# A new order of all steps and a new bank plan, with the time of each change of PE's tile mode counted

## The reference, cut to what matters

```python
x = x + tanh(g_xattn[0]) * L0_xattn(layernorm(x), ctx, ctx, ...)   # plain attention
x = x + tanh(g_ffn[0])   * L0_ffn(layernorm(x), ...)    # gelu of a linear map for the 192 best rows of 256
x = x + tanh(g_xattn[1]) * L1_xattn(ctx, ctx, layernorm(x), ...)   # plain attention
x = x + tanh(g_ffn[1])   * L1_ffn(layernorm(x), ...)    # 8 gated experts (top 2) and a shared one of twice the width
x = x + tanh(g_xattn[2]) * L2_xattn(layernorm(x), ctx, ...)        # causal attention
x = x + tanh(g_ffn[2])   * L2_ffn(layernorm(x), ...)    # 8 experts of 512 hidden units (top 2) and a shared one
x = x + tanh(g_xattn[3]) * L3_xattn(layernorm(x), ctx, ctx, ...)   # only the 51 best queries of each head
x = x + tanh(g_ffn[3])   * L3_ffn(layernorm(x), ...)    # rows and weight rounded to a 6-bit grid, then linear
```

## Time and profile before

| | |
|---|---|
| time, median of 3 runs | 957.2 us (955.71 to 961.45) |
| span of the profiled execution | 952.6 us |
| PE busy | 873.0 us (92%), 7,897 matmul records |
| PEld busy | 604.0 us (63%) |
| DVE busy | 712.2 us (75%) |
| ACT busy | 639.3 us (67%) |
| POOL busy | 497.5 us (52%) |
| chain that ended last | PE 64%, DVE 16%, POOL 7%, ACT 6%, issue 5% |

### The profile page before, as it was taken

The page is one execution under the profiler, slowest core; times in us unless marked ns, Lnnn a source line. Parts: engine busy times, 40 slices in busy tenths (PEclk is TensorE's granted clock), DMA queues, the critical chain, the costliest instruction groups (busy, mean ns, idle before and its releaser), DMA issues.

```text
span 952.6 us, 22448 instructions
## 1 busy us (share of the span) xinstructions
PE 873.0 (92%) x7897; PEld 604.0 (63%) x7897; DVE 712.2 (75%) x2174; ACT 639.3 (67%) x1460; POOL 497.5 (52%) x627
## 2 busy tenths in 40 slices
PE   6798889999999999899987999999999999999963
PEld 3344347855799987478533365746588987887522
DVE  7997988878543378987998899897745357656887
ACT  2786667767774645798674767777797448777841
POOL 6446555775962234655366265557772525533172
PEclk7897999999999999999998899999999999999997
DMA  5433241221100010002102021111110010000000
GB/s 156 111 96 86 73 111 43 77 64 37 28 23 23 14 39 3 21 24 63 36 21 74 20 66 32 32 41 30 33 41 1 18 35 1 19 20 18 20 3 24
DMA packets 67519, 39.93 MB, mean 42 GB/s; under 512 B 8263, under 2 KB 65376, under 8 KB 67408
## 3 DMA queue, kind: packets, MB, share of 16 engines
q1 hardware_dynamic: 62608, 30.44, 12.5%
q0 software_dynamic: 2208, 6.78, 2.6%
q10 hardware_dynamic: 2592, 1.26, 0.5%
HBM read 11.12 MB, written 1.05 MB: 13 GB/s over the span
## 4 chain that ended last, share of the span: by engine, by line
PE 64%; DVE 16%; POOL 7%; ACT 6%; issue 5%; DMA 1%; SPq 0%; DVEq 0%; ACTq 0%; POOLq 0%
PE banks L1062 12%; PE banks L1053 12%; PE banks L886 8%; PE banks L1022 6%; DVE mx L1364 6%; PE banks L868 4%; PE banks L845 4%; PE banks L831 3%; PE banks L1032 3%; ACT probs L743 3%; POOL h L603 3%; PE banks L991 2%; PE banks L824 2%; POOL rn L650 2%; PE banks L931 2%
## 5 line engine op out<-in xcount | busy, mean ns | idle before, releaser
L1364 DVE TENSOR_REDUCE mx<-banks 128x4 f32<-128x1024 f32 (+1 forms) x240 | 284.1, 1217 | 25.9 <-PE banks L845 18.9
L743 ACT ACTIVATE probs<-banks 128x512 f32<-128x512 f32 (+1 forms) x512 | 258.7, 582 | 53.3 <-PE banks L868 50.2
L796 ACT ACTIVATE probs<-banks,b_sb 128x256 f32<-128x256 f32 x288 | 118.0, 474 | 72.8 <-PE banks L1053 71.3
L886 PE MATMUL banks<-probs,v_aug 128*9 128x256 f32 (+1 forms) x2048 | 149.1, 373 | 7.2 <-ACT probs L743 5.9
L1062 PE MATMUL banks<-w_sb,probs 128*128 128x128 f32 x1152 | 140.6, 277 | 0.2 <-ACT probs L743 0.2
L1062 PEld LDWEIGHTS banks<-w_sb,probs 128*128 128x128 f32 x1152 | 134.9, 192 | 5.7 <-issue 2.5
L1053 PE MATMUL banks<-hT,w_sb 128*128 128x256 f32 x576 | 137.4, 382 | 0.1
L596 POOL TENSOR_TENSOR rstd<-veps,mhalf 128x2 f32<-128x2 f32 x64 | 46.2, 723 | 165.5 <-DVE veps L1311 164.8
L650 POOL TENSOR_TENSOR rn<-ss,mhalf 128x32 f32<-128x32 f32 x16 | 88.0, 5500 | 53.2 <-DVE ss L1159 52.9
L1053 PEld LDWEIGHTS banks<-hT,w_sb 128*128 128x128 f32 x576 | 104.4, 190 | 14.7 <-DVE xs L1235 0.8
L845 PE MATMUL banks<-k_st,q_st 64*128 64x256 bf16 (+1 forms) x1024 | 93.4, 277 | 14.3 <-DVE mx L1364 4.6
(11 more groups left out here) (195 smaller groups left out, 1451.5 us busy)
## 6 DMA issues: line engine op xcount, KB each, us to landing
k_st<-k_parts SPq DMA_DIRECT2D x192, 64.0 KB, 2.1
q_st<-q_parts SPq DMA_DIRECT2D x186, 64.0 KB, 2.1
w_sb<-in_w POOLq DMA_DIRECT2D x16, 256.0 KB, 3.3
fc_sb<-in_fc POOLq DMA_DIRECT2D x6, 256.0 KB, 4.1
x_in<-in_x SPq DMA_DIRECT2D x8, 128.0 KB, 4.3
cT<-in_ctxT SPq DMA_DIRECT2D x8, 128.0 KB, 2.7
out_x<-xs SPq DMA_DIRECT2D x8, 128.0 KB, 2.0
q_st<-mT SPq DMA_DIRECT2D x32, 16.0 KB
```

Of the source, the lines that this page charges most:

```text
L743: nc.scalar.activation(probs[s][:, part % UNIT_RING, 2 * a:2 * a + 2, 0:n], b_bank(w, a + 1)[:, 0:2 * n].rearrange("p (j q) -> p j q", j=2 ...
L796: ins = nc.scalar.activation(hid[s][:, part % UNIT_RING, c, :], b_bank(w, half + 1)[:, j * ROWS:(j + 1) * ROWS], ACT.Gelu, bias=b1_sb[:, p ...
L886: ins = nc.tensor.matmul(c_bank(b, l, u // 4)[VW * i:VW * i + VR, g % 2, q0:ROWS], v_aug[s][:, t, 4 * g + i, :], probs[s][:, u % UNIT_RING ...
L1364: nc.vector.tensor_reduce(mx[s][:, r, :, hp0:hp0 + n], banks[:, first:first + 2, :].rearrange("p a (n k) -> p a n k", n=n), AX.X, ALU.max) ...
```

## The change

Both strings of digits are replaced, `TURNS_TAKEN` and `BANKS_TAKEN`; no other line differs. There is the same number of steps, instructions, bytes and waits of every kind. The ACT_TABLE_LOADs of ACT, which the build puts in where the kind of function changes, are 43 in place of 45. What made the digits, a planner outside the kernel that now counts the time of each change of tile mode, is not in the file. The first lines of each:

```diff
 TURNS_TAKEN = """
-0002012001311331020003100000202003000101213111001100110011001101200210202020120120023101212121122322
+0001103021231201000032100002330000000110211301101100101010111100200120202001301202022220111212113123
...
 BANKS_TAKEN = """
-1023546012345671002345671023456701253406712503456703124056341203567401236740123406123456701234560123
+3046170124523674130167512645672345106723115674023154670523404536072314562371674521673401673254013567
...
```

More of the change, by code:

```diff
@@ L152 @@
-6774465467557477776777776777777547775545667766765775774645666776764767767457444466764576774455554454
-4665477676556566656654656565665564666464665777777567656756676657757776746766547556645776777776657477
-4577577767767675775776574777677657475765474564757775647646777647546477767777745757654677
+0001103021231201000032100002330000000110211301101100101010111100200120202001301202022220111212113123
+1102121020130313311001201022112021320032000012122201030332332231231102021121112331212323323100133300
+2210330123033302020323232013232222010313200033000120101201031100130303133003033310003201331101121201
@@ new lines @@
+2113212113222210002100001100221223221220322321220311230221212330012300322022131010021110102013110210
+1002211212210213322102111221212221031303310130330331213003320222303222330222103333101213213310103133
+0100202201201200221201102333331300121032121032123301212100212203012212200130303312213100120012302001
+1022013333000210111100010001211111200211000321201013222021201011001022010000020002101120212131111211
+2011102020101001120321210113111112122203130210300212202202332020202012202320003230210311211222311002
@@ new lines @@
+2223200020120310303001002320100030313000103031000123213002032203313112132130203313013221301211233111
+3111311212211121133131031113233103112323230230333300001220331232220131002330031001023311311031103044
+1114111343333412341132222553353525424343433454432342224432434444343222352224535234223555444544552554
+4452455253435423324433244554335453554254543343545223545454455334434424525435543343354235253323532345
+3323353223532455226536335335335363356545644443635443445343354656364364464646644664464366464635644534
@@ new lines @@
+5334436336466663334363656566644636454563366465546345665633776447766545665656444447654666455566744646
+4445575765755757767757774457775744766445455755756777467657776675457775554655575564577555765745576575
+7754765555466565456746676564654666446746677776776475646466647565557647466467445666565466746645766666
+6666667566754456676544745754676757747554544755554667556776747677646775476576744445447676444455767555
+4464465454474755664744557547774547557656654747454476676575767757564476754577777665657474766776756464
@@ L155 @@
+7575546775675544644457446675454455644445777645467775545765756657557675545547465677554647455777756466
+6466667564744665747456774744466676765656777677646555767666466574577446754654456775554677554566574766
+7446464577567577747674477776777775774676776766767755776656776467677577665445646557776447744545554546
+6646745475674556655665566555646656646646677576765765776676656767675776677746755645674747577676745657
+7774747777577477775767677656477745577476474756577766564565777774656776777777656574657477
 """
@@ L214 @@
 BANKS_TAKEN = """
-1023546012345671002345671023456701253406712503456703124056341203567401236740123406123456701234560123
[L216 to L233, removed]
+3046170124523674130167512645672345106723115674023154670523404536072314562371674521673401673254013567
+3456017402534012356147230514763024615234756246023571452341562437025416234016234670541234750163427016
@@ new lines @@
+4672346743206754120537463215642376450167230456307467142501476537432014532701237456013274523107145701
+5263472501423164523016427452301745671245036704521037612504356120437502143502347160524310761352076352
+4576123045623145601427360512367031567201546720123451206703402167214016376234015623470132645720175426
+1052451024561304612540764210674276027361523643165413412634012643056201576340153274105261374210526410
+3524167052461352745301657241650421706417365417352140612456701253467125043016745201452367045671234057
@@ new lines @@
+2605346721543671205731052376104762304703472763402731456012435612456123547623450176234515623472567172
+1034651201627637142350764317625140243710273514703250435213042571327564312046723502367153401267521461
+2401256743012345670324531231675423545612075621237601456730124517042670145236752312407430124573601263
+7245731624352063125704511245123450145120456712756312437560423701453601734561037126546712465301425632
+1756013276542034563201564723705613047564125637042360562416532406542370156245602356012345607127063124
@@ new lines @@
+5603710345612753016245316230145672403672013505674235047635620312576045627430127356103215672350167234
+0533417563213741560234125603403246013542037650145712416756071205601245670124562310456120560143243651
+2746501346701675342601273462071264031724021753042451571243670367213407671043167310672341074526451730
+5634150234167320457106324105641207352047125073642510301235641273456127037651342657341202570673125673
+4372645173054123764502375604237053641230423154326752301423750613425073460213456012365046231610326450
@@ L234 @@
+1462143051720653012407563425671250346123456041345251063430531054132350761405372154375723451675134766
+710672345101673545260317620415732415374020176350426135470
 """
```

## The result

The changed kernel takes 968.4 us (median of 4 runs, 965.45 to 975.35), the kernel before beside it 957.2: ratio 1.0109, 95% interval 1.0062 to 1.0155. So it is about 1% slower, 8 to 11 us, and outside the range of 942 to 967. The forecast was a small gain.

The account below looks back on a forecast made before the run. PE was taken to bound 50 to 475 and 550 to 900 us, DVE the rest. Terms -1.4 - 2.1 - 1.9 - 0.9 + 0.5 - 0.5 + 3.4 = -2.9 us from 957.2 gave 954 us, range 942 to 967.

Parts of the forecast that it names:

- Price of a mode change: On PE, each change of tile mode costs 0.10 us; 14 fewer changes give -1.4 us.
- The waits named: PE's waits at turns: three in PE-bound stretches, together -1.9 us; batch 5's in the DVE-bound middle, -0.9 us.
- The -0.5 at the end: Near the end, three turns ahead of three affine3 remove PE's 0.47 us wait for ACT's copy: -0.5 us.
- the -2.1 for short chains: Missing PE work between the two PE steps of short chains falls from 82.5 to 80.4 us: -2.1 us.
- the 0 for the ACT tables: On ACT, two fewer table loads of 1.283 us gain 0; -2.6 us if ACT had been waited for.
- Start: +0.5: At the start, first maxima tile comes 1.5 to 3 us later, some turns and norms earlier: +0.5 us, between -1 and +3.
- +3.4 for the PE-bound stretches: Banks retaken too early there: missing time grows by 6.8 us, half taken as paid, +3.4, bounds 0 and +6.8.
- Rival (b): Banks taken too early decide: 16.5 us extra missing time paid in full, DVE-bound stretches as well; 967 us, chance 0.16.
- my static count: Bank takes with less PE work than the reading time; after maxima tiles 26 before, 51 after, missing 6.0 to 16.8 us.
- What would show it: Signs in the changed profile: PE idle 27 to 31 us in PE-bound stretches, named turn waits shorter, clock not falling there.

Follow-up runs that it names:

- the probe: Kernel before with one extra one-column matmul in each of 72 hidden steps: whole-array 975.8 us, 64-row tile (144 mode changes more) 994.6 us.
- f5: Changed order, each output's bank chosen anew by the read times in the changed kernel's trace; 954.7 us, ratio to the kernel before 0.9920.
- i4: Changed order, all banks chosen by the later read times of two traces, the changed kernel's and f5's; ratio to the kernel before 0.9956.
- h2: Order of the kernel before, banks chosen by the read times of its own trace; ratio to the kernel before 1.0006.
- e4: Kernel before with one step moved, the query of batch 0 behind the keys of batch 1; ratio to the kernel before 1.0021.
- i3: Changed kernel with f5's banks only from 70 to 476 and 595 to 901 us, the PE-bound stretches; ratio to the kernel before 1.0039.
- h4: Changed kernel with f5's banks in the first 96 steps (55 us) only; ratio to the kernel before 1.0038.
- i1: Changed kernel with f5's banks from 70 us on only, its own banks before that; ratio to the kernel before 0.9972.
- i2: Changed kernel with f5's banks only in the middle stretch, 484 to 601 us; ratio to the kernel before 1.0073.
- e3: Changed order, each output given the bank longest free by a count of PE's work with fixed reader times; 983.5 us, ratio to the kernel before 1.0235.
- h3: Order of the kernel before, banks that leave 31.8 us missing by its trace in place of 12.4; ratio to the kernel before 1.0109.

## Why the prediction was wrong, point by point

**Price of a mode change: right, a little small.** In the changed kernel's trace sixteen matmuls of line 1062 take 1.78 us ahead of a whole-array step and 1.88 ahead of the 9 rows of line 1047:

```profile
282.26 1.95 PE L1062 MATMUL banks<-w_sb,probs 128*128 128x128 f32 x16
284.14 0.71 PE L1047 MATMUL banks<-b_sb,resid 9*128 9x128 f32 x4
...
288.34 1.95 PE L1062 MATMUL banks<-w_sb,probs 128*128 128x128 f32 x16
290.12 0.60 PE L898 MATMUL banks<-cT,wqk 128*128 128x256 f32 x2
```

With the probe's 0.13, 14 changes are worth 1.8 us and not 1.4. The Trainium skill, TensorEngine Tiling (Array Packing), section Key Properties, says that a change of tiling mode drains the engine; the probes agree that it costs, and put it at 0.13 us.

**The waits named: right.** The turns that waited 1.37, 0.60, 0.86 and (the one in the middle) 1.82 us in the earlier trace rows, and the long wait of the earlier trace rows, in order of time:

```profile
79.97 0.44 PE L824 MATMUL banks<-ident,h 128*128 128x128 f32 x2 [0.58 <-POOL h L603]
...
222.33 0.44 PE L824 MATMUL banks<-ident,h 128*128 128x128 f32 x2
...
535.69 0.44 PE L824 MATMUL banks<-ident,h 128*128 128x128 f32 x2 [0.72 <-POOL h L603]
...
678.83 0.38 PE L824 MATMUL banks<-ident,h 128*128 128x128 f32 x2
...
956.76 1.12 PE L824 MATMUL banks<-ident,h 128*128 128x128 f32 x4 [7.60 <-POOL h L645]
...
961.75 0.71 PE L1070 MATMUL banks<-w3T,hT 128*128 128x128 f32 x4 [0.47 <-ACT hT L674]
```

The first three fell to 0.58, 0 and 0, the middle one to 0.72: 0.79 + 0.60 + 0.86 + 1.10 = 3.4 us less, where 1.9 + 0.9 = 2.8 was forecast. The one near the end stayed (8.08, now 7.60). The -0.5 at the end came too: from the turn that ended this wait to the end of PE's last matmul it took 6.4 us before (the row below is its last) and takes 5.7, though a wait of 0.47 for ACT's copy is still there.

```profile
947.93 1.69 PE L1070 MATMUL banks<-w3T,hT 128*128 128x128 f32 x8
```

All terms but the banks made -6.3 us. f5 against the kernel before is -0.8%, -7.7 us (interval -4.5 to -10.7), i4 -4.2; both have fewer bank waits than the kernel before as well. Against h2, whose waits are nearest to theirs, they are -8 and -5 us. So the sum of the order's terms fits, though no run tells them apart: the -2.1 for short chains and the 0 for the ACT tables were not tested alone.

**Start: +0.5, measured about +2** (e4, 1.0021, 0 to 4 us by its interval; 1.2 us of lag in f5). Within its bounds of -1 and +3.

**Banks: the step that failed.** The text took +3.4 for the PE-bound stretches, "since a bank wait is free where PE would wait for a chain anyway", and nothing for the others, since "most are where DVE sets the pace". Measured against f5 the changed banks cost 16 us (against i4 12.7). f5's own waits are 5.7 us fewer than in the kernel before; the 13.9 us by which the waits grew from the kernel before are, at 0.7 to 0.9, some 10 to 12 us, about three times the term. In the PE-bound stretches i3 gives 4.7 us, inside the bounds of 0 and 6.8 and not to be told from the 3.4 that I took. At the start h4 and i1 give 5 us where the sum had nothing. The reason is in the rows: where DVE sets the pace, its work is what PE writes. A tile whose bank is still queued at DVE can only be written once DVE has read it, and then DVE has nothing for the time of writing. DVE-bound is no cover for a wait of PE on DVE's own input. This is shown for the start; for the middle, i2's 1.4 us leaves it open, and the end was not tried.

**Rival (b) came nearest**: full payment, in the DVE-bound stretches as well, 967 us. It had 0.16 because I took the missing time of my static count at face value and then halved it; the measured waits grew by 13.9 us, near its 16.5. Its time is 1.4 us from the measured one; that all of it is paid in full is more than the runs show. The upper bounds of the forecast's own terms, added up, come to +13 us or 970, so the range of 967 was cut below them.

**What would show it**: a wait between the second and third tile came (1.00 us); PE's idle time in the PE-bound stretches was 34.9 us, between the 27 to 31 of the forecast and the 40 of (b); the clock stayed at 0.98 and 1.00 there. The turns of batch 6 and batch 0 waited 0 and 0.58 us, under the 0.3 and 1.0 named. The forecast was to be wrong if the waits in the PE-bound stretches moved by more than 8 us or the clock fell in one of them. Neither happened, they rose by 4.9, and the forecast was wrong all the same: the test looked where the sum had put the banks' price and not at the start, where the sum had put none.

## To carry to other kernels

When a buffer or bank plan changes, count for each reuse how long the last reader takes to get to it in a trace, its queue included, and price the missing time at most of its length (here 0.7 us for each, over twelve kernels), also where the reader is the bound: it starves if its writer waits for it. A plan by distance or by fixed reader times can look better and be worse (e3, a loss of 2.4% in place of 1%); a plan by the read times of the order's own trace turned a loss of 1% into a gain of 0.8%, and a second such plan into 0.4%, with not one step moved. Where the banks were well spread already, it won nothing (h2).

## What was unexpected of the hardware

Part of the lag in the changed kernel's profile need not be work of the change. Between 120 and 160 us the granted clock was 1.00 in the profiled execution of the kernel before, 0.83 and 0.91 in that of the changed kernel, and the same 0.83 and 0.91 in h3, which has the order of the kernel before. i2 runs the same instructions on the same banks as the changed kernel up to 485 us. Four tables by stretch, before, changed, h3, i2:

```profile
120.00:140.00 20.00, 17.01 (x167) 8.97 (x166) 18.09 (x51) 13.84 (x31) 12.57 (x19) 1.00 0.43 111
140.00:160.00 20.00, 18.80 (x194) 12.34 (x195) 15.37 (x32) 14.36 (x34) 6.97 (x11) 1.00 0.15 33
```

```profile
120.00:140.00 20.00, 16.96 (x162) 8.37 (x162) 16.14 (x48) 13.16 (x29) 10.05 (x15) 0.83 0.36 90
140.00:160.00 20.00, 17.26 (x168) 9.81 (x168) 14.10 (x38) 12.87 (x29) 4.95 (x8) 0.91 0.30 82
```

```profile
120.00:140.00 20.00, 16.70 (x145) 8.55 (x146) 15.60 (x39) 12.51 (x27) 9.05 (x14) 0.83 0.34 88
140.00:160.00 20.00, 17.95 (x178) 9.76 (x177) 14.14 (x44) 13.43 (x31) 4.25 (x7) 0.91 0.26 72
```

```profile
120.00:140.00 20.00, 16.73 (x173) 9.16 (x174) 18.36 (x51) 14.79 (x32) 11.74 (x19) 1.00 0.40 100
140.00:160.00 20.00, 18.00 (x192) 10.26 (x191) 15.55 (x47) 13.66 (x32) 6.52 (x10) 1.00 0.29 78
```

By the lag, the changed kernel loses about 4 us there against the kernel before, h3 and f5 4 to 5 (0.83 and 0.91 as well), while h1, the changed kernel once more, had 0.91 and 1.00 and lost about 2, and i2, with 1.00 and 1.00, lost nothing. PE is idle 1 to 4 us in each of these slices in all of them, and whether the clock falls differs. So single traces of the same kernel differ by some us in one stretch beside a different clock, and the verdicts above rest on the timed ratios. Why it fell in one and not in the other stays open.
